# A pipeline of scan, projections and experts with its jobs in three lanes, and one of three state additions given to a DMA issued by GpSimd

## The reference, cut to what matters

```
h   = x W^T + b + 2 (x A[idx]) B[idx]                 # "cond", low rank 16
u,g = split(h W_in^T)                                 # 2048 channels each (D)
u   = silu(causal_conv(u, 4 taps) + conv_b)
dt, Bm, Cm = split(u Wx^T); each rms-normed           # 64, 16, 16 columns
delta = softplus(dt Wdt^T + dt_bias)
state[d,n] = exp(delta[d] A[d,n]) state[d,n] + delta[d] u[d] Bm[n]     # over the 256 tokens, 16 n
y[d] = sum_n state[d,n] Cm[n] + D_param[d] u[d]
x   = x + (y silu(g)) W_out^T
x   = x + FFN(cond2(x))      # low-rank adapted base, 8 experts of rank 64, top 2 by softmax
```

## Time and profile before

| | |
|---|---|
| time, median of 3 runs | 2613.73 us (2610.88 to 2616.55) |
| the profiled execution | 2611.66 us, its span 2609.9 us |
| PE busy | 2321.2 us (89%) |
| DVE busy | 2239.9 us (86%) |
| POOL busy | 2121.8 us (81%) |
| ACT busy | 1622.4 us (62%) |
| DMA moved | 350.04 MB, 134 GB/s in the mean |

### The profile page before, as it was taken

One profiled execution on the slowest core, in us unless ns is written; L12 is line 12 of the kernel. 1 busy time (PEld: TensorE's weight loads), 2 busy tenths in 40 slices (PEclk: granted clock), 3 DMA queues, 4 the chain that ended last, 5 costly groups with the idle time before them and its releaser, 6 DMA issues.

```text
span 2609.9 us, 30425 instructions
## 1 busy us (share of the span) xinstructions
PE 2321.2 (89%) x10128; PEld 1911.7 (73%) x10128; DVE 2239.9 (86%) x2084; ACT 1622.4 (62%) x3751; POOL 2121.8 (81%) x1092
## 2 busy tenths in 40 slices
PE   8977998799989999899989999899988987786968
PEld 6866675488777878688777878688777866665857
DVE  1277777589999999999999999999999999999892
ACT  1466555466667766776667766776667766775550
POOL 0087776689889998999889998999889998999770
PEclk9988998899999999899999999899999999888989
DMA  6352433434346434543336434544336333522322
GB/s 213 125 199 85 113 105 111 129 124 137 113 127 199 140 128 131 182 145 137 113 127 199 141 128 131 182 145 137 112 107 202 126 108 101 170 92 97 121 84 97
DMA packets 131511, 350.04 MB, mean 134 GB/s; under 512 B 38609, under 2 KB 43217, under 8 KB 129883
## 3 DMA queue, kind: packets, MB, share of 16 engines
q1 hardware_dynamic: 108600, 296.18, 35.1%
q10 hardware_dynamic: 22756, 51.92, 6.0%
HBM read 337.03 MB, written 11.02 MB: 133 GB/s over the span
## 4 chain that ended last, share of the span: by engine, by line
PE 55%; POOL 14%; DVE 13%; ACT 9%; issue 7%; DMA 1%; ACTq 0%; SPq 0%; POOLq 0%; DVEq 0%
PE ubank L573 9%; PE gbank L594 8%; PE late L639 8%; DVE scan L1196 7%; POOL st L1396 6%; POOL st L1404 6%; ACT scan L1038 4%; PE gbank L603 4%; PE small L555 3%; PE late L674 3%; DVE st L1208 3%; PE late L555 3%; PE scan L573 2%; PE small L755 2%; PE late L613 2%
## 5 line engine op out<-in xcount | busy, mean ns | idle before, releaser
L1196 DVE TENSOR_TENSOR_SCAN scan<-scan,st 128x1024 f32<-128x1024 f32 x512 | 1153.4, 2285 | 192.5 <-ACT scan L1038 171.8
L1396 POOL TENSOR_TENSOR st<-w_sb,bc 128x1024 f32<-128x1024 f32 x512 | 1196.9, 2358 | 77.7 <-PE gbank L603 49.8
L1038 ACT ACTIVATE scan<-delta,A_sb 128x255 f32<-128x255 f32 x2048 | 846.5, 459 | 0.0
L1404 POOL TENSOR_TENSOR st<-st 128x1024 f32<-128x1024 f32 x256 | 603.0, 2356 | 214.9 <-DVE st L1208 204.9
L594 PE MATMUL gbank<-h,wt 128*128 128x256 f32 x2048 | 488.3, 394 | 20.1 <-DVE yg L1222 19.4
L594 PEld LDWEIGHTS gbank<-h,wt 128*128 128x128 f32 x2048 | 402.7, 198 | 93.2 <-DVE yg L1222 27.1
L1208 DVE TENSOR_TENSOR st<-scan,bc 128x1024 f32<-128x1024 f32 x384 | 455.2, 1213 | 0.0
L573 PE MATMUL ubank<-h,wt 128*128 128x256 f32 x1712 | 419.2, 401 | 0.0
L639 PE MATMUL late<-yg,wt 128*128 128x256 f32 x1792 | 401.2, 382 | 0.0
L1035 ACT ACTIVATE scan<-iota 128x4 f32<-128x4 f32 x512 | 86.6, 169 | 501.3 <-DVE st L1208 455.9
L573 PEld LDWEIGHTS ubank<-h,wt 128*128 128x128 f32 x1712 | 348.1, 204 | 58.2 <-issue 3.6
(11 more groups left out here) (193 smaller groups left out, 2445.7 us busy)
## 6 DMA issues: line engine op xcount, KB each, us to landing
wt<-in_W_in SPq DMA_DIRECT2D x256, 512.0 KB, 3.7
wt<-in_W_out SPq DMA_DIRECT2D x128, 512.0 KB, 3.3
wt<-in_cond_W SPq DMA_DIRECT2D x64, 512.0 KB, 3.6
bc<-bc_rows ACTq DMA_DIRECT2D x64, 512.0 KB, 6.5
wt<-G_tiles SPq DMA_DIRECT2D x32, 512.0 KB, 3.7
wt<-in_ffn_B SPq DMA_DIRECT2D x32, 512.0 KB, 3.4
xb<-in_x SPq DMA_DIRECT2D x8, 1024.0 KB, 6.2
x<-in_x ACTq DMA_DIRECT2D x28, 256.0 KB, 3.6
```

The costliest lines, as they stand in the source:

```text
L1038: last = fn(t[:, k, 1:T], delta[:, c, 1:T], ACT.Exp, scale=A_sb[:, col:col + 1])
L1196: v_.tensor_tensor_scan(Tps[q % 2][:, :], Tps[q % 2][:, :], x_, 0.0, ALU.mult, ALU.add).then_inc(scan_done, 1)
L1396: tt(st[:, n % ST_RING, :, :], w_sb[:, i % 2:i % 2 + 1, :].to_broadcast([P, NQ, T]), bc[:, 0, q * NQ:(q + 1) * NQ, :], ALU.mult).then_inc( ...
L1404: tt(st[:, n % ST_RING, :, :], st[:, n % ST_RING, :, :], st[:, (n - 1) % ST_RING, :, :], ALU.add).then_inc(add_done, 1)
```

## The change

The side jobs now stand in three lanes. `late_job` keeps bank `late`, `small_job` and `end_job` keep bank `small`, and a new lane, `half_job`, has the upper half of `gbank` with its own pair of counters. Most cond chunks and the last quarter of the expert output, cut into two halves ("Bs", 6 and 7), go to the half lane. On PE the late and small job come ahead of sum_states, and the gate projection moves from `gbank` to the upper half of `ubank`: sum_states no longer waits for the gate's silu but for `yg_done` of the slot before, and the gate waits for the readers of the slot before it (`ubank_free`).

The conv taps now accumulate in `cv`, a new SBUF tile, so a tap reads `up` and `cv`, both in SBUF, and no PSUM. They are made one slot later, between mul 1 and scan 2; on ACT the copies that feed them (`u_evac`, L899 and L900 before) stand one slot later too, behind decay(i, 2) and ahead of decay(i, 3). The y sum and gate product move behind mul 3. ACT's gate silu comes after decay(i, 3). The softmax's small steps are spread over slot 11.

mul 1 now writes its plane in SBUF like the others. `add_first` is gone; in its place GpSimd issues `add_dma(i)`, a DMA that reads plane 4i (512 KB) and accumulates it into plane 4i+1, behind dbu(i+1, 0). dbu(i+1, 1) follows, then GpSimd waits for the DMA's landing (`acc_st`) before dbu(i+1, 2), whose plane is the one that the DMA reads.

In sequence 0 the three folding jobs use the gate weights as 8 more columns of the same matmuls (264 and 256 columns in place of 8 and 512), and the bias job's copy has a stage tile of its own and no longer waits for the b2 store.

```diff
+def late_job(i):
+
+    b, c = split(i)
+    if b == 0:
+        return {13: ("g", 0, 7), 14: ("b2", 0, 0), 15: ("bias", 0, 0)}.get(c)
+    f = b - 1
+    if c == 0:
+        return ("B", f - 1, 2) if f else None
+    if c <= 8:
+        return ("wout", f, c - 1)
+    if c == 9:
+        return ("la2", f, 0)
+    if c in (10, 11):
+        return ("A", f, c - 10)
+    if c in (12, 13):
+        return ("wb", f, c - 12)
+    return ("B", f, c - 14)
...
+def small_job(i):
 
     b, c = split(i)
     if c == 13 and b < LAST:
         return ("ms", b + 1, 0)
-    if c == 15 and b < LAST:
-        return ("dt", b + 1, 2)
+    if c in (14, 15) and b < LAST:
+        return ("dt", b + 1, c - 13)
     if b == 0:
...
+            return ("dt", 0, c + 2)
+        return ("g", 0, c - 6) if c <= 12 else None
+    f, j = b - 1, b + 2
     if c <= 4:
         return ("dt", b, c + 3)
-    if c in (9, 10, 11):
-        return (("lg", "wT", "wb")[c - 9], b - 1, 0)
+    if c in (6, 9) and j < B:
+        return ("cond", j, {6: 3, 9: 6}[c])
+    if c in (10, 11):
+        return (("lg", "wT")[c - 10], f, 0)
+    if c in (14, 15):
+        return ("B", f, {14: 3, 15: 2}[c])
...
+def half_job(i):
 
     b, c = split(i)
-    if c == 12 and b < LAST:
-        return ("xp", b + 1, 0)
-    if c == 13 and b < LAST:
-        return ("dt", b + 1, 0)
     if b == 0:
         if c == 2:
             return ("la", 2, 0)
-        if 3 <= c <= 10:
-            return ("cond", 2, c - 3)
-        if c == 14:
-            return ("b2", 0, 0)
-        if c == 15:
-            return ("bias", 0, 0)
-        return None
+        return ("cond", 2, c - 3) if 3 <= c <= 10 else None
...
+    if c == 0:
+        return ("la", 3, 0) if f == 0 else ("Bs", f - 1, 7)
+    if j < B and c in (1, 3, 5, 7, 8, 9):
+        return ("cond", j, {1: 0, 3: 1, 5: 2, 7: 4, 8: 5, 9: 7}[c])
     if c == 14 and b + 3 < B:
         return ("la", b + 3, 0)
-    if b == 0:
-        if 6 <= c <= 12:
-            return ("g", 0, c - 6)
-        if c == 15:
-            return ("g", 0, 7)
-        return None
...
         def u_home(v):
             if v < NC:
                 return quarter(v % 4)
-            if NC <= v < NC + 10 and v % 2:
-                return small[:, :]
-            return ubank[:, :]
+            return late if NC <= v < NC + 10 and v % 2 else ubank
+
+        def cv_home(v):
+            return quarter(v % 4)[:, T:2 * T] if v < NC else cv[:, v % 2, :]
...
+            def ubank_free(i):
+
+                pe.wait_ge(q_done, i + 1)
+                if i:
+                    for v in u_chunks(i - 1):
+                        pe.wait_ge(u_ev, v + 1)
+                    if part_job(i - 1):
+                        part, k = part_job(i - 1)
+                        pe.wait_ge(part_ev, PAIRS * part + k + 1)
 
             def gate_chunk(i):
                 b, c = split(i)
                 n = TILE_NO[("gate", i, 0)]
                 if i == 0:
-                    pe.wait_ge(pc_ev, KH + 2)
-                if i >= 2:
-                    pe.wait_ge(yg_done, i - 1)
+                    pe.wait_ge(pc_ev, KH + 3)
                 pe.wait_ge(*loaded(n))
                 for k in range(KH):
-                    last = mm(gbank[:, 0:T], wt[:, n % W_RING, k, :], h0[:, b % 3, k, :],
+                    last = mm(ubank[:, T:2 * T], wt[:, n % W_RING, k, :], h0[:, b % 3, k, :],
                               start=(k == 0), stop=(k == KH - 1))
                 last.then_inc(gate_mm, 1)
...
             def sum_states(i):
                 pe.wait_ge(add_done, 3 * i + 3)
-                pe.wait_ge(q_done, min(i + 2, CHUNKS))
+                if i:
+                    pe.wait_ge(yg_done, i)
+                else:
+                    pe.wait_ge(pc_ev, 2 * KH)
+                if takes_half(i):
+                    pe.wait_ge(*emptied(takes_half(i)))
+                if part_job(i):
+                    part, k = part_job(i)
+                    pe.wait_ge(part_ev, PAIRS * part + k + 1)
...
+                if late_job(i):
+                    run(late_job(i), i)
+                if small_job(i):
+                    run(small_job(i), i)
                 if i:
                     sum_states(i - 1)
-                if first_job(i):
-                    run(first_job(i), i)
+                if half_job(i):
+                    run(half_job(i), i)
                 if i == 0:
                     for m in range(4, KH):
                         pro_cond(1, m)
-                if us:
-                    if us[0] % NC == 0:
-                        h0_ready(us[0] // NC)
-                    pe.wait_ge(u_done, us[0])
-                    u_chunk(us[0])
-                if part_job(i):
-                    out_part(*part_job(i))
-                if late_job(i):
-                    run(late_job(i), i)
-                if len(us) > 1:
-                    if first_job(i):
-                        pe.wait_ge(*emptied(first_job(i)))
-                    u_chunk(us[1])
-                if last_job(i):
-                    run(last_job(i), i)
+                ubank_free(i)
+                for v in us:
+                    if v % NC == 0:
+                        h0_ready(v // NC)
+                    u_chunk(v)
                 if i + 1 < CHUNKS:
                     gate_chunk(i + 1)
+                if end_job(i):
+                    run(end_job(i), i)
+                if part_job(i):
+                    out_part(*part_job(i), i)
...
-                act.wait_ge(gate_mm, i + 1)
-                if i >= 2:
-                    act.wait_ge(yg_done, i - 1)
-                fn(qg[:, i % 2, :], gbank[:, 0:T], ACT.Silu).then_inc(q_done, 1)
-                fn_exp_table()
-                if job and job[0] == "ms":
-                    evac(job)
                 decay(i, 2)
                 if c == 15 and b < LAST:
                     load_C(b + 1, 0)
+                act.wait_ge(gate_mm, i + 1)
+                if i:
+                    for v in u_chunks(i - 1):
+                        u_evac(v)
+                    if half_job(i - 1) and half_job(i - 1)[0] != "Bs":
+                        act.wait_ge(yg_done, i - 1)
+                        evac(half_job(i - 1), i)
...
                 decay(i, 3)
                 if c == 15 and b < LAST:
                     load_C(b + 1, 1)
                     load_B(b + 1, 3)
-                if job and job[0] in ("dt", "wT"):
-                    evac(job)
-                for v in us:
-                    u_evac(v)
+                if i >= 2:
+                    act.wait_ge(yg_done, i - 1)
+                if i and part_job(i - 1):
+                    part, k = part_job(i - 1)
+                    act.wait_ge(part_ev, PAIRS * part + k + 1)
+                fn(qg[:, i % 2, :], ubank[:, T:2 * T], ACT.Silu).then_inc(q_done, 1)
+                if i:
+                    for v in u_chunks(i - 1):
+                        u_silu(v)
+                fn_exp_table()
...
-                v_.scalar_tensor_tensor(cv, up[:, e, k:k + T], cw[:, c, k:k + 1], cv, ALU.mult, ALU.add
+                v_.scalar_tensor_tensor(cv_home(v), up[:, e, k:k + T], cw[:, c, k:k + 1], cv_home(v), ALU.mult, ALU.add
                                         ).then_inc(conv_step, 1)
...
-                if q == 1:
-                    v_.tensor_tensor(Tps[1][:, :], Tps[1][:, :], cq, ALU.mult).then_inc(prod_done, 1)
-                else:
-                    v_.tensor_tensor(plane(n), Tps[q % 2][:, :], cq, ALU.mult).then_inc(mul_done, 1)
-
-            def add_first(i):
-                dve.wait_ge(prod_done, i + 1)
-                dve.wait_ge(mul_done, 4 * i + 1)
-                v_.tensor_tensor(plane(4 * i + 1), Tps[1][:, :], plane(4 * i), ALU.add).then_inc(mul_done, 1)
+                v_.tensor_tensor(plane(n), Tps[q % 2][:, :], cq, ALU.mult).then_inc(mul_done, 1)
 
             def y_sum(i):
                 dve.wait_ge(id_mm, i + 1)
...
                 scan(i, 0)
-                between(i)
+                if i:
+                    take_late(i - 1)
+                if weigh:
+                    soft_max_step(b - 1, 0)
                 scan(i, 1)
-                between2(i)
+                if i:
+                    take_rest(i - 1)
+                if weigh:
+                    soft_max_step(b - 1, 1)
                 mul(i, 0)
+                if weigh:
+                    soft_max_step(b - 1, 2)
                 mul(i, 1)
-                add_first(i)
-                if b and c == 9:
-                    soft_max_in(b - 1)
+                if weigh:
+                    soft_max_step(b - 1, 3)
+                if weigh:
+                    soft_max_step(b - 1, 4)
+                if i:
+                    for v in u_chunks(i - 1):
+                        for k in range(TAPS - 1):
+                            conv_tap(v, k)
+                if weigh:
+                    soft_max_step(b - 1, 5)
                 scan(i, 2)
```

(85 more changed lines are left out.)

400 lines of the change are left out of this document (188 added, 212 removed).

## The result

The changed kernel takes 2895.8 us (2890.4 to 2900.3, 4 runs) against 2613.2 us: 1.108 times as long, interval 1.1055 to 1.1104 (95%). The forecast was 2910 us. The profiled execution has a span of 2891.7 us, 281.8 more than before.

A forecast was written before the change was run, and what follows sets the result against it. POOL was to bound the changed kernel at 21.2 us a slot. From 2611.7 us: +267 (slots 17 to 107), +34 (last 18), +10 (start), -15 (bias job), 2 to the median: 2910 us, range 2720 to 3110.

The forecast's parts named there:

- the last 18: Slots behind slot 107, without taps: 19.6 us each against 18.0, +34 us in all.
- T: Accumulating DMA, start of issue to landing: 5.5 us between 3.3 and 7.4; POOL's slot becomes 14.22 + T.
- POOL's hold by the taps: SBUF taps and POOL's instructions exclude each other; POOL loses up to 1.46 us a slot, upper end taken.
- no blocking: Rival at the conv taps: T still 5.5, POOL's slot 19.7 us, total about 2770 us; chance 0.15.
- The cast as the model of a tap: DVE's 16-element cast, median 1666 ns against 175 with POOL idle, taken as nearest row for SBUF taps.
- POOL alone sets the slot: In slots 17 to 107, POOL's loop with DMA and blocked taps gives 21.2 us a slot, against 18.26.
- DVE's new wait on ACT: Ahead of the taps DVE waits 1.6 us a slot for ACT's copies; costs nothing while POOL's slot is 19 or more.
- DVE busy well under the slot: Sign of the forecast: DVE and PE busy well under POOL's slot of 21 us.
- PE's clock: Granted 0.97 in the middle; longer slots make PE sparser, but PE, at 17.06 us a slot, is not the bound.
- the long transfer: Rival: T of 7.4 or more, each us costing 123 us; 7.4 gives 3145 us; chance 0.10.
- the bias job: In the slots around 15 and 16, its copy no longer waits 12.66 us for a store: -15 us, ends 0 and -30.
- The lanes cost nothing: Lanes and split expert output: same matmuls, cost 0, ends 0 and 0.5 us a slot, hidden below POOL.

The follow-up runs named there:

- e2: Kernel before with the first addition done by GpSimd's accumulating DMA; taps stay in PSUM, old order of jobs: 2804 us, ratio 1.075.
- e1: Kernel before with the conv taps accumulating in SBUF instead of PSUM; order, waits and DMAs unchanged: 2949 us, ratio 1.130.
- e3: Changed kernel with the first addition back on DVE and no DMA from GpSimd; lanes and SBUF taps stay: 2810 us, ratio 1.076.
- e9: Changed kernel with taps accumulating in PSUM again, in the u matmul's half bank; DMA, lanes and order stay: 2786 us, ratio 1.067.
- e4: Changed kernel with the accumulating DMA replaced by a plain copy of the same plane, losing the first two products' sum: 2830 us, ratio 1.083.
- e7: Kernel before with one of three taps reading its second operand from SBUF and writing PSUM: 2676 us, ratio 1.024.
- e12: Changed kernel with ACT's copies for the taps moved ahead of decay(i, 2): 2831 us, ratio 1.085.
- e10: Changed kernel with the first addition on DVE, taps in PSUM and ACT's copies ahead of decay(i, 2): 2536 us, ratio 0.971.
- e5: Kernel before with the DMA for the first addition, GpSimd adding plane 2 into plane 3 before waiting for the landing: 2763 us, ratio 1.057.

## Why the prediction was right

The direction and both causes held: the DMA and the blocked taps each make the kernel slower when put in alone (e2, e1), the changed kernel gets faster when either is taken out (e3, e9), and a shorter landing gives time back (e4). By places, predicted and measured: slots 17 to 107 +267 and +268.5; the last 18 +34 and +29.7; what lies before chunk 18, -5 and -17.3; the end, 0 and +0.9. POOL's slot of 21.2 was met by 21.21, and 19.6 without taps by 19.65.

That the slot agrees to 0.1 us is luck: its terms were off and cancelled. Slots 17 to 107 by stretch (columns as in the earlier trace rows), of the kernel before, of the changed kernel and of e9:

```profile
537.02:2198.70 1661.68, 1532.01 (x6860) 1287.04 (x6859) 1582.56 (x1472) 1136.94 (x2639) 1506.51 (x773) 0.97 0.43 140
...
519.77:2449.91 1930.14, 1604.78 (x6850) 1334.54 (x6850) 1784.90 (x1386) 1134.42 (x2643) 1620.42 (x866) 0.92 0.50 145
...
493.90:2338.14 1844.24, 1557.19 (x6838) 1305.62 (x6837) 1479.13 (x1385) 1120.54 (x2637) 1587.41 (x866) 0.93 0.52 152
```

| POOL, us a slot | predicted | changed | e9 |
|---|---|---|---|
| its work before | 16.58 | 16.56 | 16.56 |
| the issue | 0.88 | 0.88 | 0.88 |
| wait for the landing | 2.26 | 2.77 | 2.54 |
| hold by the taps | 1.46 | 0.37 | 0 |
| waits for DVE and PE | 0 | 0.39 | 0.04 |
| gaps between its instructions | 0 | 0.24 | 0.24 |
| slot | 21.18 | 21.21 | 20.27 |

The prediction has issue and wait as one term, 3.14; it is split here by the issue's measured 0.88. In these slots POOL waits 252.5 us for the landing in the changed kernel and 230.9 in e9.

- *T, 5.5 us.* Mis-sized. The median is 5.4, but a slot goes by the mean, and single landings take up to 10.8. Issue, dbu and wait of slots 17 to 107 add up to 0.88 + 2.36 + 2.77 = 6.0 us.
- *POOL's hold by the taps, 1.46 us a slot.* Mis-sized. dbu takes 2447 ns against 2358 before, but 2425 in e9 as well, where no tap is blocked; there the record of the dbu behind the DMA's issue begins 0.26 us ahead of the issue's end. What the taps add is the difference of POOL's busy time, 17.81 - 17.44 = 0.37. The taps hit DVE, not POOL: 3 x (1579 - 486) = 3.3 us a slot, where I had 5. In the slot they cost 21.21 - 20.27 = 0.94 us (e9), for 1.5 predicted.
- *Nothing but POOL's loop without the taps.* 19.7 was predicted and e9 has 20.27; the gaps of 0.24, which the kernel before has too, were not in the sum. The rival "no blocking" with 2770 us was near: e9 took 2786.
- *The cast as the model of a tap.* Its rows show that a DVE instruction can be held, but a cast reads one operand, `tix` in SBUF, so it is no case of two SBUF reads. That a tap with two is held is shown by e7; why a cast with one is held too, no run shows.
- *POOL alone sets the slot.* Only half right, and with it the step that DVE's new wait on ACT costs nothing. DVE's 19.6 us of busy time and 1.44 of wait for the copies fill the slot of 21.21 as well; the sign "DVE busy well under the slot" did not come. I reckoned that DVE and POOL would arrive together, and yet priced each as if the other had room. e12 takes DVE's wait away and gains 65 us. e4 takes 1.8 us off the median landing and gains 66, where 123 us for each us of T would give about 220. The wait was as sized: 1.5 us, for 1.6.
- *PE's clock.* As predicted, PE does not bound. In slots 17 to 107 PE was busy 92% of the time at a mean granted clock of 0.97 before, 83% at 0.92 after (a mean between its two levels, 1.2 and 2.4 GHz); its work grew from 16.84 to 17.63 us a slot, well under 21.21.
- *Arithmetic.* 1.9 x 123 on top of 2910 is 3144, not 3145, and this lies above the range's end of 3110, so the range did not take in the long transfer's lower edge. At a T of 4.4 the same 123 us give 2775, not 2790.
- *The first 18 slots.* I had +10 for the start and -15 for the bias job. e9 and e10 reach chunk 18 at 493.9 and 489.2 us against 537.0, so the new order gains 43 to 48 us there, and the blocked taps take 26 of them back (519.8 in the changed kernel). Whether it is the shorter wait of the earlier trace rows, the folding jobs on fewer matmuls or the lanes was not separated.
- *The lanes cost nothing.* Right, and they are worth more than I gave: beside SBUF taps, 140 us (e1 against e3). How much of e10's gain is due to the copies' early place is open: no run has the lanes with PSUM taps, no DMA and the copies late.

On the two rules weighed: with two SBUF reads a tap waits for a POOL instruction that reads SBUF, as the Trainium skill says ("SBUF — State Buffer", section "Who interferes with whom"); e7's rows agree, 1679 ns against 490. Its fit for such a DMA ("DMA: Bandwidth & Descriptors", section "Anatomy of one DMA — SWDGE (gpsimd) path") gives 3.2 us for 512 KB, an estimate; the plain copy landed in 3.6, the accumulating one in 5.4, so for the latter the measurement decides, and even the estimate of 4.4 by both operands' bytes is short.

## What to carry to other kernels

Moving work from the busiest engine to the third busiest pays only by the slack between them, and an asynchronous helper costs its issuer the issue and the exposed part of the landing: count both against that slack (here 0.88 and 2.4 us on POOL against 1.22 saved on DVE). Covering the landing is not enough if it makes other work late: e5 took the wait away and was still 150 us slower than before. When an operand moves from PSUM to SBUF, look at how many SBUF operands the DVE instruction then reads and whether GpSimd runs beside it: here a tap of 0.49 us took what was left of a POOL instruction of 0.7 to 2.4 us, and 0.28 more. Test the parts of a bundled change one by one: of this one, two parts cost 338 and 193 us alone in the old order, and the rest, with the copies early, gained 77.

## What the runs showed of the hardware that was not expected

- An accumulating DMA of 512 KB from SBUF to SBUF takes the 16 DMA engines for 12.6% of 2891.7 us, the plain copy (e4) for 5.9% of 2837.7: 2.2 times the engine time for the same 67.12 MB, and 5.4 against 3.6 us to landing. Its issue occupies POOL for 878 ns against 593.
- POOL's instruction right behind such an issue begins before the issue's record ends. In e9:

```profile
1406.14 0.87 POOL L1456 DMA_DIRECT2D st<-st  x1
1406.75 2.64 POOL L1450 TENSOR_TENSOR st<-w_sb,bc 128x1024 f32<-128x1024 f32 x1
```

  From 1407.01, the issue's end, to 1409.39 are 2.38 us, a plain dbu: its longer record is overlap and no loss.
- A held tap ends 0.28 us behind the POOL instruction that held it, and the next POOL instruction starts before that. Holding is nearly one-sided: DVE lost 3.3 us a slot, POOL 0.37.
